# Edge counts in place of a normalised adjacency in the graph experts, as products of two float32r parts

## The reference, cut to what matters

```python
def _L3_gnn_ref(x, gate_W, gate_b, Wl, bl, Wr, edge_index):
    src, dst = (edge_index[0], edge_index[1])
    gates = jax.nn.softmax(x @ gate_W + gate_b, axis=-1)
    top_v, top_i = jax.lax.top_k(gates, TOP_K)                      # 2 of 4 experts
    deg = jax.ops.segment_sum(jnp.ones((src.shape[0],), x.dtype), dst, num_segments=n)
    inv_deg = jnp.where(deg > 0, 1.0 / jnp.maximum(deg, 1.0), 0.0)[:, None]

    def sage_conv(h, W_l, b_l, W_r):
        aggr = jax.ops.segment_sum(h[src], dst, num_segments=n) * inv_deg
        return aggr @ W_l + b_l + h @ W_r
    ...
    for e in range(NUM_EXPERTS):
        h = x
        for l in range(LAYERS):
            h = jax.nn.relu(sage_conv(h, Wl[e, l], bl[e, l], Wr[e, l]))
```

## Time and profile before

| | us |
|---|---|
| median of three runs | 2063.62 |
| the three runs | 2059.88, 2063.62, 2067.06 |
| span of the profiled execution | 2061.2 |
| PE busy in that span | 1922.7 |
| DVE, ACT, POOL busy | 926.4, 501.0, 320.8 |
| graph experts, first product to last (1515.2 to 1808.6) | 293.4 |

### The profile page before, as it was taken

The page is one execution under the profiler, slowest core; times in us unless marked ns, Lnnn a source line. Parts: engine busy times, 40 slices in busy tenths (PEclk is TensorE's granted clock), DMA queues, the critical chain, the costliest instruction groups (busy, mean ns, idle before and its releaser), DMA issues. The chain is left out here.

```text
span 2061.2 us, 27279 instructions
## 1 busy us (share of the span) xinstructions
PE 1922.7 (93%) x8940; PEld 1038.7 (50%) x8967; DVE 926.4 (45%) x2848; ACT 501.0 (24%) x1382; POOL 320.8 (16%) x342
## 2 busy tenths in 40 slices
PE   8998997999989999999999799888799999979999
PEld 4454455777645434543553333334334444458877
DVE  7464455000069886997799510175321111140012
ACT  0152351111134352234225321155110000010000
POOL 0000000333317403720570000000000000010001
PEclk9999998999989999999999999999899999999999
DMA  4003009998268505720677399772440220079984
GB/s 163 1 1 103 1 11 352 399 358 318 83 207 250 147 1 189 210 79 6 185 203 264 116 332 386 294 234 79 138 174 0 87 87 0 0 286 403 338 306 160
DMA packets 180664, 358.00 MB, mean 174 GB/s; under 512 B 28816, under 2 KB 38304, under 8 KB 180524
## 3 DMA queue, kind: packets, MB, share of 16 engines
q1 hardware_dynamic: 157548, 285.94, 38.4%
q0 software_dynamic: 22976, 70.23, 11.5%
HBM read 334.43 MB, written 21.69 MB: 173 GB/s over the span
## 5 line engine op out<-in xcount | busy, mean ns | idle before, releaser
L1099 PEld LDWEIGHTS ps<-tokT,w 128*128 128x128 f32 x2304 | 259.8, 192 | 10.7 <-issue 6.7
L1099 PE MATMUL ps<-tokT,w 128*128 128x128 f32 x2304 | 260.6, 275 | 3.1 <-DVE tokT L1244 3.1
L1557 POOL DMA_INDIRECT w<-xl_d,src_i x216 | 215.0, 995 | 296.6 <-DMA xl_d<-XL 228.5
L1653 PE MATMUL ps<-XP,wide 128*128 (+1 forms) x456 | 185.8, 508 | 0.2 <-DVE XP L1915 0.2
L1658 PE MATMUL ps<-w,ident 128*128 128x512 f32 x270 | 141.4, 605 | 9.7 <-DMA w<-xl_d,src_i 9.3
L1322 POOL DMA_INDIRECT spread_d<-N,slot x12 | 11.8, 983 | 693.4 <-DVE slot L1203 690.4
L1653 PEld LDWEIGHTS ps<-XP,wide 128*128 128x128 f32 x456 | 81.5, 189 | 73.5 <-issue 67.1
L1768 ACT ACTIVATE wide<-oht 128x128 fp32r<-128x128 bf16 x228 | 68.1, 308 | 199.2 <-PE ps L1658 179.3
L1118 PE MATMUL ps<-w,O 128*128 128x512 f32 x256 | 111.2, 592 | 0.0
L1930 DVE SCALAR_TENSOR_TENSOR w<-ps,w 128x512 f32<-128x512 f32 x144 | 98.0, 681 | 5.5 <-PE ps L1658 5.2
L1258 DVE TENSOR_TENSOR hT<-act,ps 128x512 f32<-128x512 f32 x20 | 13.8, 688 | 178.9 <-ACT act L1151 178.9
(11 more groups left out here) (510 smaller groups left out, 3032.8 us busy)
## 6 DMA issues: line engine op xcount, KB each, us to landing
w<-L_ffn_W SPq DMA_DIRECT2D x16, 2048.0 KB, 12.7
w<-L_ffn_W SPq DMA_DIRECT2D x8, 4096.0 KB, 17.2
w<-fc1T SPq DMA_DIRECT2D x32, 1024.0 KB, 14.2
w<-fc2T SPq DMA_DIRECT2D x30, 1024.0 KB, 14.2
w<-L_ffn_w_gate SPq DMA_DIRECT2D x20, 1024.0 KB, 9.3
w<-L_ffn_w_up SPq DMA_DIRECT2D x20, 1024.0 KB, 12.0
w<-L_ffn_w_down SPq DMA_DIRECT2D x10, 2048.0 KB, 15.3
w<-L_ffn_w SPq DMA_DIRECT2D x8, 2048.0 KB, 13.9
```

The costliest lines, as they stand in the source:

```text
L1099: m = pe.matmul(k.ps[:, 1 + (q * ins + i) % 4, s * P:(s + 1) * P], self.W1[u][i][:, f, (q * T + s) * P:(q * T + s + 1) * P], self.tokT[:, ...
L1557: gp.indirect_dma_start(self.G[:, u, :], None, k.xl_d, bass.IndirectOffsetOnAxis(ap=k.src_i[:, i:i + 1].bitcast(U32), axis=0)).then_inc(k. ...
L1653: m = pe.matmul(bank, self.wide[:, i % DEEP, :], self.XP[:, q].rearrange("p t n -> p (t n)")[:, bass.ds(at, D)], start=False, stop=(q == 1 ...
```

## The change

The counts C stay in SBUF to the graph experts, in float32r (a four-byte format that DVE and ACT can write and TensorE can read), and Cn is gone. A value that meets C is split into two float32r parts: `hi` is the value rounded to float32r, `lo` what is left of it, so that hi*C + lo*C stands for the f32 product. The degree's division comes behind the sum.

- In the head, the four products with `diag` (L416), the four writes of `diag` (L429) and the four multiplications into `Cn` (L438) leave the first attention. The key columns' banks now wait for C's copies.
- At the entry of the graph experts the gate's products come first, behind the wait for all of NT; then `ones` times `diag` (written there now) spreads the inverse degrees, and ACT copies them to `inv_row`; then comes NT times Wr of expert 0, the own-row product (`own`), with the gate's four turns behind its first bank; only then the neighbour sums, 16 matmuls with `hi` and 16 with `lo`, three banks for four tiles. DVE multiplies each by `inv_row` into A0. ACT no longer copies A0.
- In each expert the sum over the edges is 16 matmuls with `hi` and 16 with `lo`, into banks 4 to 7. DVE makes `hi` and `lo` from the banks where it copied PR, adds the bias to the own-row banks 0 to 3 while the edges are summed, and then for each tile multiplies the sum by the inverse degree and adds (one instruction), applies ReLU and gate weight, adds to X. For experts 1 to 3, H1 times Wl now waits for the end of the previous expert (`heads`), since its banks hold that expert's sums.
- SP loads Wr ahead of Wl in each layer, and the first Wr has a semaphore of its own (`rooted`).

```diff
     def means(self, v, ch):
-        v.wait_ge(self.diagonal.sem, self.diagonal.at(1))
         for t in range(T):
-            last = v.tensor_tensor(k.Cn[:, t, :], k.C[:, t, :], k.ps[:, 7, :], ALU.mult)
-        last.then_inc(self.summed.sem, 1)
...
                 columns(0, W[0])
-                if counts is not None:
-                    counts.tensor(pe)
...
             def _(pe):
                 norm.tensor(pe)
+                norm.wait_cols(pe)
+                r.products(pe, 7)
+                pe.wait_ge(spread.sem, spread.at(1))
                 for t in range(T):
-                    for f in range(T):
-                        m = pe.matmul(k.ps[:, T + t, :], k.N[:, f, t * P:(t + 1) * P], k.Cn[:, f, :], start=(f == 0),
-                                      stop=(f == T - 1))
-                    m.then_inc(neighbors.sem, 1)
-                norm.wait_cols(pe)
-                r.tensor(pe, 3)
+                    m = pe.matmul(k.ps[:, T, t * P:(t + 1) * P], k.ones[:], diag[:, t, :], start=True, stop=True)
+                m.then_inc(rowed.sem, 1)
...
+                def means():
+                    for t in range(T):
...
+                        if t == T - 1:
+                            pe.wait_ge(meant.sem, meant.at(1))
+                        for part in (hi, lo):
+                            for s in range(T):
+                                m = pe.matmul(k.ps[:, T + t % 3, :], part[:, s, t * P:(t + 1) * P], k.C[:, s, :],
+                                              start=(part is hi and s == 0), stop=(part is lo and s == T - 1))
...
+                        pe.wait_ge(rooted.sem, rooted.at(16))
+                        own(u, 0, True)
+                        r.turns(pe, 7)
+                        for t in range(1, T):
+                            own(u, t, True)
+                        means()
...
                     for t in range(T):
-                        for s in range(T):
-                            m = pe.matmul(k.ps[:, t, :], k.Cn[:, s, t * P:(t + 1) * P], PR[:, s, :],
-                                          start=False, stop=(s == T - 1))
+                        for part in (hi, lo):
+                            for s in range(T):
+                                m = pe.matmul(k.ps[:, T + t, :], k.C[:, s, t * P:(t + 1) * P], part[:, s, :],
+                                              start=(part is hi and s == 0), stop=(part is lo and s == T - 1))
                         m.then_inc(k.out.sem, 1)
...
                     for t in range(T):
                         v.wait_ge(k.tp.sem, k.tp.at(t + 1) + e * T)
-                        m = v.tensor_copy(PR[:, t, :], k.ps[:, T + t, :])
+                        ch.link(v.tensor_copy(hi[:, t, :], k.ps[:, T + t, :]))
+                        m = v.tensor_tensor(lo[:, t, :], k.ps[:, T + t, :], hi[:, t, :].bitcast(F32), ALU.subtract)
...
                         v.wait_ge(k.out.sem, k.out.at(t + 1) + e * T)
-                        v.tensor_tensor(o[:, t, :], k.ps[:, t, :], b1[u][:], ALU.add).then_inc(emptied.sem, 1)
-                        v.wait_ge(emptied.sem, emptied.at(t + 1) + e * T)
+                        ch.link(v.scalar_tensor_tensor(o[:, t, :], k.ps[:, T + t, :], k.inv_deg[:, t:t + 1],
+                                                       o[:, t, :], ALU.mult, ALU.add))
```

More of the change, by code:

```diff
@@ L408, in scalar @@
             a.activation(k.C[:, t, :], k.ps[:, T + t, :], ACT.Copy).then_inc(self.copied.sem, 1)
[L410 to L417, removed]
     def degrees(self, v, ch):
@@ L450, in done @@
     def done(self):
-        done((self.summed, 2), (self.copied, T), (self.spread, 1), (self.diagonal, 1))
+        done((self.summed, 1), (self.copied, T))
 def keep_busy(pe, k, bank, n):
@@ L848, in tensor, with turns @@
         m.then_inc(k.gate_mm.sem, 1)
+    def turns(self, pe, bank=0):
+        k, width = self.k, self.width
         pe.wait_ge(k.gate_rows.sem, k.gate_rows.at(1))
@@ L853, in tensor @@
         m.then_inc(k.gate_turned.sem, 1)
+    def tensor(self, pe, bank=0):
+        self.products(pe, bank)
+        self.turns(pe, bank)
     def vector(self, v, bank=0, chosen=None):
@@ L2865, in sage @@
         norm = Norm(k, c, k.X, k.N, k.NT)
-        neighbors, meant, emptied = signals(c, k, "neighbors", "meant", "sage_emptied")
+        diag, inv_row = sb(c, k, "diag", [P, T, P]), sb(c, k, "inv_row", [P, N])
+        neighbors, meant, emptied, parted, spread, rowed, inverse, rooted = signals(
+            c, k, "neighbors", "meant", "sage_emptied", "rows_parted", "degrees_spread", "degrees_rowed", "inverse_row",
+            "root_weights")
         with nc.Block() as block:
@@ L2899, in step @@
                             pe.wait_ge(emptied.sem, emptied.at(t + 1) + (e - 1) * T)
+                            own(u, t, True)
+                        for f in range(T):
+                            if not later(e, 1) and t == 0:
+                                pe.wait_ge(meant.sem, meant.at(f + 1))
+                            m = pe.matmul(k.ps[:, t, :], W[u][0][:, f, t * P:(t + 1) * P], A0[:, f, :],
+                                          start=False, stop=(f == T - 1))
+                        m.then_inc(k.mm.sem, 1)
+                    if later(e, 1):
+                        pe.wait_ge(k.heads.sem, k.heads.at(1) + (e - 1))
+                    for t in range(T):
                         if not later(e, 1) and t == T - 1:
                             pe.wait_ge(k.gate_ready.sem, k.gate_ready.at(1))
-                        for w, x in ((W[u][0], A0), (W[u][1], k.NT)):
-                            for f in range(T):
[L2904 to L2907, removed]
                         for f in range(T):
@@ L2925, in _ @@
                 norm.scalar(a)
-                for t in range(T):
-                    a.wait_ge(neighbors.sem, neighbors.at(t + 1))
-                    a.activation(A0[:, t, :], k.ps[:, T + t, :], ACT.Copy).then_inc(meant.sem, 1)
-                r.scalar(a, 3)
+                a.wait_ge(rowed.sem, rowed.at(1))
+                a.activation(inv_row[:], k.ps[:, T, :], ACT.Copy).then_inc(inverse.sem, 1)
+                r.scalar(a, 7)
                 def step(e, u, j):
```

83 lines of the change are left out of this document (56 added, 27 removed).

## The result

The changed kernel takes 2033.99 us (median of four runs, 2033.36 to 2036.62), the kernel before, run beside it, 2065.05: a ratio of 0.9857, interval 0.9842 to 0.9872. Forecast were 2033.1 us. The profiled execution of the changed kernel has a span of 2031.8 us against 2061.2, 29.4 less.

The account below looks back on a forecast made before the run. PE, busy 93% of the span, was taken to bound the kernel, matmuls alone through the experts. -31.4 + 0.35 + 1.39 - 0.89 = -30.55 us took the median 2063.62 to 2033.1 us, range 2027 to 2041.

Parts of the forecast that it names:

- The products: Neighbour sums and four experts' edge sums: 32 float32r matmuls at 0.233 us, 7.46 instead of 13.74 each; five gain 31.4 us.
- The higher bound: Edge products: charging the first load's 0.43 us to the float32r matmul costs some 0.2 more per product start, 1.0 in all.
- The lower bound: Edge products: columns alone set 0.2145 us, half an f32 record, 3.0 us better; as the rival of shorter loads, 2030.1, chance 0.05.
- rival that no load hides: Edge products: each matmul costs 0.405 us, a product 12.95, five gain only 4.0; 2060.5 us, chance 0.04.
- The split: DVE's cast and subtraction of each expert's last tile, 1.4 us, hidden behind PE's 13.74 us of H1 times Wr.
- The last tile: End of the last expert: DVE at 1.98 us a tile falls behind PE's 1.86, +0.35 us.
- The entry: Start of the graph experts, without its product: +1.34 NT wait, -0.84 logits' wait, +0.89 products with diag, sum +1.39 us.
- The wait for NT: Entry: the gate now needs NT's last copy, so PE waits from 1515.25 to 1516.59, +1.34 us.
- the vanished wait for the logits: Entry: PE's wait for the logits from 1532.51 to 1533.35 goes, -0.84 us.
- What I said of the own rows: Entry: without the own rows ahead, PE would wait some 2 us for DVE's split of N, at most 0.69 an instruction.
- The head: First attention: the products with diag leave PE between query and key columns, 0.89 us gained, all of it showing.
- that rival: Lower clock, 1.2 GHz, through all five edge products: a product 14.94 us, the kernel 2070.5, chance 0.03.

Follow-up runs that it names:

- e1: Changed kernel with C and both parts in f32, one f32 product in each edge product, the new order kept: 2064.81 us, ratio to the kernel before 1.0007.
- e7: Changed kernel with 64 stationary columns loaded instead of 128 in the experts' edge sums, part of the sums left out: 2037.24 us, one run.
- e10: Changed kernel with 32 stationary columns loaded instead of 128 in the experts' edge sums, part of the sums left out: 2032.87 us, one run.
- e9: Changed kernel with each matmul of the experts' edge sums cut into two of 256 moving columns, so twice the loads: 2032.81 us, one run.
- e2: Changed kernel with C, hi and lo in float16 instead of float32r: 2031.12 us, ratio to the kernel before 0.9841.
- e6: Changed kernel with the DVE subtraction that makes lo done three times over: 2036.85 us, ratio to the kernel before 0.9872.
- e3: Changed kernel with the first expert's own rows behind the neighbour sums instead of ahead: 2035.28 us, ratio to the kernel before 0.9860.
- e5: Changed kernel with four unused f32 products put back between query and key columns of the first attention: 2033.68 us, ratio to the kernel before 0.9851.
- e0: The changed kernel once more, unaltered, for a second profile: 2033.39 us, ratio to the kernel before 0.9851.

## Why the forecast held, step by step

**The products.** 13.74 to 7.46 each, as forecast, and e1 shows that nothing else carries the gain. The higher bound, an extra 0.2 at each start, was not there: the first load's 0.43 lies in the shadow of the f32 record. The lower bound, 0.2145 by the columns, was built on a wrong step. I took a float32r column to cost half of an f32 record's and the load to set the 0.233, so that shorter loads would win 3.0 us; e7, e10 and e9 show that no load would. The price came from three loads of the same type and shape and held; the reason that I gave for it fell. The rival that no load hides (2060.5) fell too, at 7.46 a product where it had 12.95. By the Trainium skill ("TensorE: Matmul & The Clock Gate", section on the back-to-back gap), the gap of a matmul of 512 columns, taken by itself, is some 216 ns. The trace agrees for float16 (0.2155 in e2) and does not for float32r (0.2333).

**The split.** Hidden, as forecast; e6 made it twice as long and the block stayed.

**The last tile.** DVE's last tile but one, and the start of the last, on its timeline:

```profile
1777.13 0.75 DVE L3003 SCALAR_TENSOR_TENSOR o<-ps,inv_deg,o 128x512 f32<-128x512 f32 x1
1777.91 0.49 DVE L3005 TENSOR_SCALAR o<-o,wE 128x512 f32<-128x512 f32 x1
1778.44 0.69 DVE L3007 TENSOR_TENSOR X<-X,o 128x512 f32<-128x512 f32 x1
1779.05 0.75 DVE L3003 SCALAR_TENSOR_TENSOR o<-ps,inv_deg,o 128x512 f32<-128x512 f32 x1
```

A tile takes 1779.05 - 1777.13 = 1.92 and not 1.98: the next one starts 0.08 before the addition ends, which I had as 0.04 behind it. Against PE's 1.87 that is 0.05 a tile, 0.15 in all, and the last tile's three lasted 1.99 (to the block's end at 1781.04) where they took 1.95. That makes +0.2. Measured whole it is +0.27 in place of +0.35: from the last expert's H1 times Wl (it starts at 1743.70, before at 1767.26) to the block's end it is 37.34 where 43.35 was, 6.01 less and not 6.28. The rest is mostly the start: DVE takes up the first tile 0.26 behind the end of PE's stream for it (1773.04 to 1773.30), where its last one started 0.20 behind (1794.73 + 13.73 = 1808.46 to 1808.66).

**The entry.** Forecast +1.39 without its product. From the first copy of NT to the end of expert 0's first layer it was 1561.26 - 1515.24 = 46.02 and is 1556.51 - 1515.17 = 41.34: 4.68 less, product included, where 1.39 - 6.28 = -4.89 was forecast, 0.21 off. PE loses 0.10 four times, each time where matmuls of another shape follow: behind the gate (1516.52 + 8 x 0.429 = 1519.95, next at 1520.05), behind the products with `diag` (0.99 to the next one's start and not 0.89), in front of the turns, and behind them. The kernel before lost as much twice, in front of the gate (1515.25 + 13.73 = 1528.98, next at 1529.08) and behind the turns; two more make the 0.21. The rows of single groups don't hold this cost, and no run shows what it is. The wait for NT (1.35) and the vanished wait for the logits came as forecast. What I said of the own rows was wrong in size and cause (e3): the casts of N out of SBUF take 0.36 each and not 0.69, so the split is in time, and the 0.95 is a wait for ACT.

**The head.** Forecast -0.89; it is 28.53 - 27.63 = 0.90 less, and e5 puts it back with four products.

**The sum.** Block: 4.68 at the entry and 4 x 6.28 in the experts, less 0.27, make 29.5, which is what it lost. With the head's 0.90 that is 30.4, against 30.55 forecast. The 2033.99 lies 0.9 above the forecast, within the runs' spread. The clock in the products was 1.00, so that rival fell too. One sign that the prediction named for being wrong did appear, a clock near 0.50 between 1510 and 1780: it lay over the transposes, ahead of the products, and e0 gained as much without it. The sign was drawn too wide.

## What to carry to other kernels

Price a matmul from a row of the same type and shape, not from a record of another type; here such a row gave 31 us to a few tenths. A wait in front of a product is a place for work that needs nothing of what is waited for, if an idle engine can prepare it earlier. Where executions scatter by several us, measure a change of one us between two events that enclose it, in each profile, and not by the medians.

## What the runs showed that I had not expected

- A float32r matmul took some 0.456 ns for each moving column, at 256, 384 and 512 columns; a float16 one took 0.421 at 512. Load records of 0.188 us start 0.117 apart without holding PE up.
- DVE cast f32 to float32r in 0.36 us a 128x512 tile from SBUF, and in 0.69 from PSUM.
- The profile of the changed kernel has the clock at 0.51 over the transposes at the entry, and e0's, of the same code, has not: 1.3 us from the transposes' start to the gate's (4.48 against 3.18) that come and go between executions of one kernel.
